# Second-layer heads one slot sooner, and the slots with two heads moved in a two-layer transformer kernel

## What is computed

```python
x = L0_attn_query                                   # (8, 256, 256)
xn = _layernorm(x)
x = x + _L0_attn_ref(xn, ...) + _L0_ffn_ref(xn, ...)  # 16 heads of size 128, causal mask
xn = _layernorm(x)
x = x + _L1_attn_ref(xn, ...) + _L1_ffn_ref(xn, ...)  # 16 heads of size 16, no mask
# attention, both layers: softmax(q k^T * scale) v, heads side by side, then @ Wo + bo
```

## Time and profile before

| | us |
|---|---|
| median of 3 runs | 965.71 (964.99 to 966.11) |
| the profiled execution | 964.64 |
| its span | 962.7 |
| TensorE busy | 894.1 |
| VectorE busy | 748.2 |
| ScalarE busy | 678.8 |
| GpSimd busy | 356.1 |

### The profile page before, as it was taken

How to read it: one execution, slowest core, us unless ns; L and a number is a source line. 1 busy time by engine, 2 the same in 40 slices (tenths; PEclk the granted TensorE clock), 3 DMA queues, 4 the chain that set the end, 5 groups by cost and what they waited for, 6 DMA issues and landing times.

```text
span 962.7 us, 22856 instructions
## 1 busy us (share of the span) xinstructions
PE 894.1 (93%) x8016; PEld 719.1 (75%) x8016; DVE 748.2 (78%) x2128; ACT 678.8 (71%) x1997; POOL 356.1 (37%) x653
## 2 busy tenths in 40 slices
PE   4777989899999999999999999999999999988797
PEld 2335767677888888888888888888888888866575
DVE  6886767667887888888888888888878887876576
ACT  4787786557767777677777776777677777775464
POOL 4503565424343333333333333334333332333243
PEclk9899999999999999999999999999999999999799
DMA  9343350002000100020002000200010000100000
GB/s 292 105 153 105 128 179 2 2 23 62 2 1 24 50 24 2 7 67 14 12 1 69 5 23 2 65 10 23 2 48 26 23 2 22 35 16 8 1 13 12
DMA packets 46880, 39.98 MB, mean 42 GB/s; under 512 B 4400, under 2 KB 42032, under 8 KB 46512
## 3 DMA queue, kind: packets, MB, share of 16 engines
q1 hardware_dynamic: 46768, 38.52, 13.1%
HBM read 30.11 MB, written 8.39 MB: 40 GB/s over the span
## 4 chain that ended last, share of the span: by engine, by line
PE 66%; DVE 15%; ACT 8%; issue 3%; POOL 1%; ACTq 0%; DVEq 0%; POOLq 0%
PE ps L824 36%; PE ps L944 6%; PE ps L872 5%; ACT arena L1169 4%; PE ps L845 4%; PE ps L1043 3%; PE ps L1063 3%; DVE arena L817 3%; DVE arena L818 3%; DVE arena L1329 2%; ACT arena L813 2%; PE ps L1074 2%; PE ps L907 2%; PE ps L1045 2%; PE ps L956 2%
## 5 line engine op out<-in xcount | busy, mean ns | idle before, releaser
L818 DVE SCALAR_TENSOR_TENSOR arena<-ps,bqk,arena 128x256 bf16<-128x256 f32 x416 | 187.5, 480 | 76.6 <-ACT arena L813 76.6
L813 ACT ACTIVATE arena<-ps,bqk 128x256 bf16<-128x256 f32 x416 | 177.5, 462 | 75.0 <-PE ps L1045 56.2
L817 DVE TENSOR_TENSOR arena<-ps,arena 128x512 bf16<-128x512 f32 (+1 forms) x336 | 203.4, 632 | 23.0 <-ACT arena L812 22.8
L824 PE MATMUL ps<-arena,wqkv 128*128 128x256 bf16 x1728 | 215.5, 275 | 2.4 <-DVE arena L817 2.3
L1169 ACT ACTIVATE arena<-arena,nb 128x128 f32<-128x128 f32 (+1 forms) x256 | 114.4, 448 | 125.1 <-DVE nb L1329 125.0
L1560 POOL TENSOR_SCALAR arena<-arena,rc 128x128 f32<-128x128 f32 (+1 forms) x256 | 105.5, 424 | 260.1 <-DVE rc L1358 260.0
L1567 POOL TENSOR_SCALAR arena<-arena,rc 128x256 f32<-128x256 f32 x254 | 118.2, 478 | 210.4 <-DVE rc L1362 210.4
L812 ACT ACTIVATE arena<-ps 128x512 bf16<-128x512 f32 (+1 forms) x336 | 175.2, 558 | 25.9 <-PE ps L824 13.6
L824 PEld LDWEIGHTS ps<-arena,wqkv 128*128 128x128 bf16 x1728 | 170.6, 99 | 26.0 <-DVE arena L817 1.7
L1169 ACT ACTIVATE arena<-ps,nb 128x256 f32<-128x256 f32 x256 | 119.9, 483 | 22.1 <-DVE nb L1336 22.1
L824 PE MATMUL ps<-arena 128*128 128x128 bf16 (+2 forms) x864 | 97.8, 249 | 11.5 <-DVE arena L817 7.0
(11 more groups left out here) (116 smaller groups left out, 1283.4 us busy)
## 6 DMA issues: line engine op xcount, KB each, us to landing
scratch_qk<-arena SPq DMA_DIRECT2D x28, 128.0 KB, 1.9
arena<-scratch_qk SPq DMA_DIRECT2D x84, 32.0 KB, 1.8
arena<-scratch_qk SPq DMA_DIRECT2D x42, 64.0 KB, 2.5
arena<-in_x SPq DMA_DIRECT2D x4, 512.0 KB, 10.3
arena<-in_w_gating SPq DMA_DIRECT2D x4, 512.0 KB, 8.7
arena<-in_w_q SPq DMA_DIRECT2D x4, 512.0 KB, 4.6
arena<-in_w_k SPq DMA_DIRECT2D x4, 512.0 KB, 5.6
arena<-in_w_v SPq DMA_DIRECT2D x2, 1024.0 KB, 6.7
```

What stands on the lines that cost most here:

```text
L813: return nc.scalar.activation(out, in_, ACT.Identity, bias=bias)
L817: return nc.vector.tensor_tensor(out, in_, hi, ALU.subtract)
L818: return nc.vector.scalar_tensor_tensor(out=out, in0=in_, scalar=bias, in1=hi, op0=ALU.add, op1=ALU.subtract)
L824: last = nc.tensor.matmul(out, lhsT, rhs, start=(n == 0), stop=(n == len(steps) - 1))
```

## The change

Three tables are changed, and two waits are added and one condition altered in `turn1` and `turn1_bank` to keep banks from being overwritten.

- Every second-layer head of batches 0 to 5 stands one slot earlier (27 to 42 for batch 0).
- Batch 6's heads stood two to a slot in 124, 125, 126, one in 127, two in 128 to 131, one in 132. Now 123 to 126 hold one each and 127 to 132 two each.
- Quads' attention of batches 0 to 5 moves from slots 1, 5, 9, 13 of a 16-slot round to 0, 4, 9, 12, output projections one slot behind. In batch 6 quads 24 to 27 stood in 127, 130, 133, 134 and their output projections in 128, 134, 134, 135; now 128, 130, 132, 134 and 129, 131, 133, 135.
- The turn of a second head in `BK_QK` now also waits for the exponentials of second heads' scores in that bank (head 103 for head 101's turn), and a turn in `BK_S` from slot 133 on for batch 7's q.

```diff
--- before.py
+++ after.py
@@ -642,21 +642,21 @@
             if b == LASTB:
                 return END + h // 2
             if b == LASTB - 1:
-                return start1(b) + 12 + (0, 0, 1, 1, 2, 2, 3, 4, 4, 5, 5, 6, 6, 7, 7, 8)[h]
-            return start1(b) + 12 + h
+                return start1(b) + 11 + (0, 1, 2, 3, 4, 4, 5, 5, 6, 6, 7, 7, 8, 8, 9, 9)[h]
+            return start1(b) + 11 + h
 
         def quad_slot(n):
             b, q = divmod(n, QUADS)
             if b == LASTB:
                 return END + 3 + 2 * q
             if b == LASTB - 1:
-                return start1(b) + (15, 18, 21, 22)[q]
-            return head_slot(4 * n + 3) + 2
+                return start1(b) + (16, 18, 20, 22)[q]
+            return start1(b) + (16, 20, 25, 28)[q]
 
         def out_slot(n):
             b, q = divmod(n, QUADS)
             if b == LASTB - 1:
-                return start1(b) + (16, 22, 22, 23)[q]
+                return start1(b) + (17, 19, 21, 23)[q]
             return quad_slot(n) + 1
 
         def hidden_slot(n):
@@ -697,7 +697,7 @@
 
             if n < LASTB * H1:
                 if second(n):
-                    return BK_QK if head_slot(n) + 1 < NG0 else BK_S
+                    return BK_QK if head_slot(n) < NG0 else BK_S
                 return BK_O
             if n % 2 == 0:
                 return BK_O
@@ -857,8 +857,13 @@
                     pe.wait_ge(p1_lo, before[-1] + 1)
                 if bank == BK_QK:
                     pe.wait_ge(qk0_lo, min(slot + 1, NG0))
+                    scored = [m for m in range(B * H1) if score1_bank(m) == BK_QK and head_slot(m) <= slot]
+                    if scored:
+                        pe.wait_ge(exp1, scored[-1] + 1)
                 elif bank == BK_S:
                     pe.wait_ge(p0_lo, NG0)
+                    if slot >= piece_slot(3 * LASTB):
+                        pe.wait_ge(qkv1_lo, 3 * LASTB + 1)
                 elif bank == BK_X or bank == BK_O and n >= LASTB * H1:
                     pe.wait_ge(qkv1_lo, 3 * B)
                 elif bank == BK_O:
```

## The result

| | us | against before |
|---|---|---|
| before, median of 4 runs | 965.83 (964.99 to 966.11) | |
| changed kernel, median of 4 runs | 957.10 (956.76 to 958.42) | ratio 0.9914, 95% interval 0.9896 to 0.9931 |
| the same again, beside the later experiments: before 965.27, changed | 958.68 (957.52 to 961.80) | ratio 0.9936, interval 0.9919 to 0.9953 |

A forecast was written before the change was run, and what follows sets the result against it. TensorE, busy 894.1 of 962.7 us, was taken as the bound, with winnable idle time behind slot 124. Terms 5.15 + 1.7 - 1.4 + 0.8 + 0.65 - 1.35 gave 5.5 us, hence 960.2 us, range 956.8 to 965.6.

The forecast's parts named there:

- What bounds the kernel, and where a gain can come from: Whole kernel: TensorE is full in the steady middle; reordering wins only where it idles, behind slot 124.
- The front: Slots 124 to 127: moving second heads out removes 5.15 us of waits; 1.7 us of work moves behind 128, hidden.
- The new wait in slot 128: Slot 128: head 101's turn must wait for head 103's exponential in BK_QK; 1.9 us, bounds 0.5 and 2.5.
- I add nothing there: Slot 127: with one second head it is like slot 124 before, which had no idle time; no cost.
- The net -1.4 us of slot 128: Slot 128: the new wait of 1.9 us, set against the slot's present idle time of 0.52 us.
- VectorE catching up: Slots 129 to 131: VectorE enters 129 less in arrears, so 0.8 us of waits go, bounds 0 and 2.
- output projection 25 hidden: Quad 25's projection leaves full slot 134 for 131, ahead of a 2.53 us TensorE wait; +0.65 us.
- Slot 132's second head: Slot 132: its maxima and exponentials lengthen the chain before the last projections; -1.35 us, bounds 0.5 and 1.9.
- The clock: Slots 130, 132, 133: granted clock below 1.00 costs up to 1.7, 2.9 and 2.2 us; sum leaves it unchanged.
- late keys: Slots 27, 43, ... 123: a batch's keys come too late for the slot opening with its head; 969.3, chance 0.05.
- Rival 1: Behind slot 128: two-head slots end on VectorE and ScalarE, so the tail gives the gain back; 964 to 965, chance 0.12.
- Rival 2: Behind slot 128: the low clock spreads, another 8 us at 1.2 GHz loses 4 us; about 964, chance 0.07.

The follow-up runs named there:

- the two halves of the change: Against the kernel before: new tables only for batches 0 to 5, 968.33 us (ratio 1.0027); new tables only for batch 6, 963.30 us (0.9979).
- the two filled kernels: Matmuls and transposes repeated in idle gaps: on the changed kernel, 959.94 us; on the changed kernel with late quads and output projections, 961.15 us.
- the kernel with batch 6 alone: Kernel before with only batch 6's tables changed, single heads in 124 and 125, two to a slot from 126: 963.30 us, ratio 0.9979.
- its filled copy: The named kernel with matmuls and transposes repeated where TensorE idled: kernel before, 964.24 us (ratio 0.9989); changed kernel, 959.94 us (0.9946).

## Why the prediction was right, and where it wasn't

The forecast of 5.5 us lies near the 6.6 and 8.7 measured, partly by luck: order and waits gave 4.0 us in the pair of profiles, and the clock, which the sum left out, gave 3.5.

- **What bounds the kernel, and where a gain can come from:** right. The steady slots gave nothing, the end gave it all.
- **The front, 5.15 us of idle time and 1.7 us of work, slot 128 at 857.5:** right; slot 128 starts at 856.73, 7.76 us earlier, where 6.85 was forecast. No run splits the 0.9 us on top. The mechanism (banks held by second heads) is shown by the two halves of the change, which each bring such waits back.
- **The new wait in slot 128, 1.9 us:** right in kind and size, 1.65 us. It is nearly free, though: without it the time could not be told apart.
- **The step that failed: "I add nothing there"** for slot 127. I compared it to slot 124, whose own row has no idle time, but the bill of a slot with two heads comes a slot later: before, slot 125 opened with a wait for maxima too (0.98 of its 2.92 us). Slot 128 has no q and k projection ahead of that place, so TensorE comes there 1.3 us sooner, and waits 2.48 us. The net -1.4 us of slot 128 was -3.6, and with 0.5 us more work in it the slot is 4.1 us longer.
- **VectorE catching up, 0.8 us, and output projection 25 hidden, 0.65 us:** idle time in 129 to 131 fell from 7.04 to 5.14 us, 1.9 against 1.45 forecast. The 0.65 us left out quad 26's attention, which went under a wait as well: put back late, the moved work costs 1.2 to 1.3 us without the clock.
- **Slot 132's second head, -1.35 us:** right. At the full clock slot 132 takes 7.13 us before and 8.48 in the changed kernel, 1.35 more.
- **The clock:** I left it out of the sum, and put it at "up to 1.7, 2.9 and 2.2 us" in slots 130, 132 and 133. Measured, those are 1.7, 0 and 2.1 us: in 132 the work at half clock lies under waits for other engines. By the Trainium skill's rule ("TensorE: Matmul & The Clock Gate", Part 1: The HAM clock gate), that activity releases the throttle, I had feared a loss from more idle time near slot 128. The traces agree in part: slot 128, with 4.14 us of idle time, kept 1.00 in both profiles of the changed kernel and was at 0.84 and 0.85 in the two filled kernels with the same wait of 2.48 us. In the kernel with batch 6 alone, whose slot 128 has a wait of 3.09 us in one piece, the first-layer transposes right behind took 0.88 us for 0.52.
- **Rivals:** late keys did not occur; no wait stands at the first head of a batch. Rival 1 came true in part: at the full clock slots 128 to 133 take 41.2 us before and 46.2 in the changed kernel. They are 5.0 us longer where my terms came to 2.6 (1.4 - 0.8 + 1.35, and output projection 26's 0.66), and slot 128 alone is 2.7 us longer than I had it. Rival 2's sign, a low clock in slot 128, showed in the two filled kernels with the same slot and cost 0 and 0.7 us there.

## What to carry to other kernels

When a step is doubled up in a slot of a pipeline, charge its cost to the next slot, at the first place where the in-order engine behind it is needed. Before removing a wait look at what that engine does in the order just ahead of it: here moving three steps ahead of a reciprocal that waits for another engine won more than removing the bank conflict that the profile named. Price a low clock by the length of the same slot at the full clock, not by TensorE's busy time, and set runs side by side with their mean clocks. And a move that pays only with another one (the steady slots with batch 6, the third quad with the rest) must be tested with it.

## What the runs showed of the hardware

- TensorE's granted clock fell to half behind idle time in some runs and not in others, with the same waits ahead: slot 126 was at 1.00 in the kernel before and at 0.79 in its filled copy, slot 128 at 1.00 in the changed kernel and at 0.84 in its filled copy. Runs of one kernel spread over 3 to 8 us of 960.
- A low stretch is dear only where TensorE does not wait for others: slot 133 took 8.71 us at 0.75 and 6.58 at 1.00, slot 132 took 7.13 at 0.59 and at 1.00, slot 128 10.70 at 0.84 and at 1.00.
- Over 63 runs of the kernel before, a mean clock 0.001 lower goes with 0.6 us more. It stands for 1.9 us at half the clock in a span of 963.
- Extra matmuls in the gaps, 4 to 7 us of them, raised the kernel before's mean clock from 0.985 to 0.989, and the time hardly moved.
